# Self attention with one more score bank and shared transpose banks, and matrix products without use at pauses

## The reference, cut to what matters

```python
# x [1,512,512], ctx [1,8192,512]; 16 heads of 32, D = 512
x = x + xattn(layernorm(x), ctx)          # softmax(q k^T / sqrt(32)) v, 8192 keys, then Wo
x = x + attn(layernorm(x))                # below, 512 keys
x = x + ffn(layernorm(x))                 # 8 experts, 2 per token, 512 -> 1024 -> 512

def attn(x):
    Q, K, V = (split_heads(x @ W.T) for W in (W_Q, W_K, W_V))
    Q, K = layernorm(Q, q_ln_w, q_ln_b), layernorm(K, k_ln_w, k_ln_b)
    attn = softmax(Q @ K.T / sqrt(32)); context = attn @ V
    z = context_flat @ sparse_W_V.mean(axis=2)            # one number for each row and head
    y = top_k(z, 128)  outer  sparse_W_O.mean(axis=1)
    return y @ W_O.T
```

## Time and profile before

| | us |
|---|---|
| median of 3 runs | 1608.14 (1606.55 to 1609.6) |
| the profiled execution | 1605.24 |
| its span, first to last instruction | 1603.5 |
| mean granted clock of PE | 0.973 |
| PE busy | 1507.0 |
| DVE busy | 1252.5 |
| ACT busy | 1039.9 |
| POOL busy | 410.2 |

### The profile page before, as it was taken

One profiled execution on the slowest core, in us unless ns is written; L12 is line 12 of the kernel. 1 busy time (PEld: TensorE's weight loads), 2 busy tenths in 40 slices (PEclk: granted clock), 3 DMA queues, 4 the chain that ended last, 5 costly groups with the idle time before them and its releaser, 6 DMA issues. The chain is left out here.

```text
span 1603.5 us, 23326 instructions
## 1 busy us (share of the span) xinstructions
PE 1507.0 (94%) x8494; PEld 845.5 (53%) x8494; DVE 1252.5 (78%) x1884; ACT 1039.9 (65%) x1343; POOL 410.2 (26%) x225
## 2 busy tenths in 40 slices
PE   6799999999999989999999999999988864899998
PEld 4466666666666533333333333333345631699996
DVE  5677776776777879999999999999885668477664
ACT  3366666666666778888888888888547841244441
POOL 5455545636556011404000400100005320100002
PEclk9899999999999989999999999999999986799999
DMA  4454444444544455455545445444156036399994
GB/s 183 158 197 145 171 171 139 177 161 155 179 155 152 132 145 132 113 151 165 140 123 143 121 115 123 115 123 120 38 84 128 2 128 247 106 326 348 363 340 138
DMA packets 119776, 254.55 MB, mean 159 GB/s; under 512 B 10152, under 2 KB 26536, under 8 KB 115184
## 3 DMA queue, kind: packets, MB, share of 16 engines
q1 hardware_dynamic: 117632, 248.35, 49.7%
q0 software_dynamic: 1408, 4.46, 0.9%
q10 hardware_dynamic: 624, 0.27, 0.1%
HBM read 182.26 MB, written 61.34 MB: 152 GB/s over the span
## 5 line engine op out<-in xcount | busy, mean ns | idle before, releaser
L772 ACT ACTIVATE att_pr<-b_sc 128x1024 f32<-128x1024 f32 x512 | 496.2, 1022 | 77.1 <-PE b_sc L676 77.1
L822 DVE TENSOR_TENSOR att_tot<-att_tot,att_pr 128x2048 f32<-128x2048 f32 x200 | 466.9, 2335 | 23.1 <-ACT att_pr L772 2.3
L497 DVE CUSTOM_DVE_ANT_0 ctx_size<-ctx_tot,ctx_size 128x512 f32<-128x512 f32 x512 | 332.9, 688 | 133.4 <-PE ctx_tot L411 129.7
L462 ACT ACTIVATE ctx_size<-ctx_dif 128x1024 f32<-128x1024 f32 x256 | 262.2, 1024 | 121.6 <-PE ctx_dif L411 121.6
L676 PE MATMUL b_sc<-g_stacks,att_kst 98*128 98x512 f32 x1024 | 309.1, 424 | 2.0 <-DMA att_kst<-keys_scratch 2.0
L676 PEld LDWEIGHTS b_sc<-g_stacks,att_kst 98*128 98x128 f32 x1024 | 173.8, 189 | 237.3 <-ACT att_pr L772 211.5
L690 PE MATMUL b_o<-att_pr,att_val 128*32 128x512 f32 x2048 | 273.6, 606 | 2.0 <-issue 1.9
L411 PE MATMUL ctx_dif<-ctx_k_dif,f_q_hi 32*128 32x512 f32 x512 | 128.5, 499 | 6.6 <-DVE ctx_k_sum L481 2.8
L411 PE MATMUL ctx_tot<-ctx_k_sum,f_q_hi 32*128 32x512 f32 x512 | 128.0, 497 | 0.0
L86 PE MATMUL f_proj<-f_wv_hi,g_stacks 128*128 128x512 f32 x320 | 120.8, 420 | 0.0
L86 PE MATMUL f_proj<-g_stacks,f_wk_hi 128*128 128x512 f32 x352 | 119.5, 420 | 0.5 <-DVE f_k_lo L206 0.5
(11 more groups left out here) (302 smaller groups left out, 2106.4 us busy)
## 6 DMA issues: line engine op xcount, KB each, us to landing
m_w<-in_W SPq DMA_DIRECT2D x30, 2048.0 KB, 10.6
att_kst<-keys_scratch SPq DMA_DIRECT2D x192, 256.0 KB, 3.9
f_raw<-in_ctx SPq DMA_DIRECT2D x32, 1024.0 KB, 6.1
keys_scratch<-f_k_hi SPq DMA_DIRECT2D x32, 512.0 KB, 2.8
keys_scratch<-f_k_lo SPq DMA_DIRECT2D x32, 512.0 KB, 3.2
values_scratch<-ctx_v SPq DMA_DIRECT2D x32, 512.0 KB, 3.2
att_val<-values_scratch SPq DMA_DIRECT2D x64, 256.0 KB, 2.7
rows_scratch<-mix_blank SPq DMA_DIRECT2D x1, 3840.0 KB, 23.7
```

The source lines that it names most:

```text
L462: act.activation(size[:, i % ABS, :], dif[:, :], ACT.Abs).then_inc(s_size, 1)
L497: dve.tensor_tensor_reduce(out=size[:, i % ABS, r * CH:(r + 1) * CH], in0=tot[i % 2][:, r * CH:(r + 1) * CH], in1=size[:, i % ABS, r * CH: ...
L772: act.activation(pr[:, T % SLOTS, 2 * s:2 * s + 2, :], sc[(2 * T + s) % PAIRS][:, :].rearrange("p (j q) -> p j q", j=2), ACT.Exp, scale=SC ...
L822: dve.tensor_tensor(tot[b % 2][:, :, :], so_far, pr[:, T % SLOTS, :, :], ALU.add).then_inc(s_add, 1)
```

## The change

`keep_warm` issues matrix products whose results nobody reads. It is called at the end of `project_context` (8 products of 512 columns, single-pass type), at the start of `attend_context` (16, and 4 more after `turn`; fp32, 128 columns), before and between the first `turn_rows` there (7 and 5), at the end of `self_attend` (4, fp32, 512 columns), and twice in `mix_and_route`: before the rank products (3, fp32, 512 columns) and after the last transposes (2).

In `self_attend` there are four `full` banks instead of three, three `tp` banks which the transposes of the sums share in turn (`turned` lists who gets a bank in which order), one `o` bank, and no `rs`. ACT's list becomes exp(i), copy(i-2). The head that DVE copies is j = 1. `invert` and PE's `shares` come one step earlier in their lists, ACT's `shares` two and `take` five. The last `shares` runs before the last `weighted`.

```diff
+def keep_warm(pe, out, left, right, times):
+    for _ in range(times):
+        pe.matmul(out, left, right, start=True, stop=True)
...
+            pe.wait_ge(s_size, STEPS)
+            keep_warm(pe, dif[:, 0:CH], c.wv_hi[:, 0, 0:P], c.wv_hi[:, 0, :], 8)
...
+            keep_warm(pe, den[:, 0:P], c.ident[:, :], c.ident[:, :], 16)
             pe.wait_ge(s_shift, 4)
             turn(pe, sc[0])
+            keep_warm(pe, den[:, 0:P], c.ident[:, :], c.ident[:, :], 4)
...
+            keep_warm(pe, den[:, 0:P], c.ident[:, :], c.ident[:, :], 7)
             turn_rows(0)
+            keep_warm(pe, den[:, 0:P], c.ident[:, :], c.ident[:, :], 5)
             turn_rows(1)
...
-    FULL = 3
+    FULL = 4
     KEPT = 3
+    BANKS = 3
+    LAG = 2
+    LATE = HG + 1
...
-        tp = [pb(f"tp{n}", [P, N]) for n in range(2)]
-        o = [pb(f"o{n}", [P, N]) for n in range(2)]
-        rs = pb("rs", [P, N])
+        tp = [pb(f"tp{n}", [P, N]) for n in range(BANKS)]
+        o = pb("o", [P, N])
...
         def by_vector(i):
-            return i % HG == HG - 1
+            return i % HG == 1
...
+        turned = []
+        for i in range(ALL):
+            turned.append(("head", i))
+            if i % STEPS == 1 and i > STEPS:
+                turned.append(("share", i // STEPS - 1))
+        turned.append(("share", G - 1))
+        def bank(kind, n):
+            return tp[turned.index((kind, n)) % BANKS]
+        def bank_free(engine, kind, n):
+            at = turned.index((kind, n)) - BANKS
+            if at >= 0:
+                kind, n = turned[at]
+                if kind == "head":
+                    moved_out(engine, n)
+                else:
+                    engine.wait_ge(s_share, n + 1)
...
             def turn(i):
                 pe.wait_ge(s_exp, i + 1)
-                if i >= 2:
-                    moved_out(pe, i - 2)
+                bank_free(pe, "head", i)
...
             def weighted(unit):
-                if t == 0 and g >= 2:
-                    pe.wait_ge(s_take, g - 1)
+                if t == 0 and g >= 1:
+                    pe.wait_ge(s_take, g)
...
                 turn(i)
-                if i % HG == 1 and i > HG:
-                    weighted(i // HG - 1)
-                if i % STEPS == 2 and i > STEPS:
+                if i % STEPS == 1 and i > STEPS:
                     shares(i // STEPS - 1)
+                if i >= LATE and (i - LATE) % HG == 0:
+                    weighted((i - LATE) // HG)
+            shares(G - 1)
             weighted(G * NT - 1)
-            shares(G - 1)
+            keep_warm(pe, full[0][:, :], c.swvT[:, 0, 0:P], c.swvT[:, 0, :], 4)
...
-                if i and not by_vector(i - 1):
-                    move(i - 1)
-                if i % STEPS == 4 and i > STEPS:
+                if i >= LAG and not by_vector(i - LAG):
+                    move(i - LAG)
+                if i % STEPS == 2 and i > STEPS:
                     shares(i // STEPS - 1)
+            for i in range(ALL - LAG, ALL):
+                move(i)
...
-                if n % STEPS == 2 and n > STEPS:
+                if n % STEPS == 1 and n > STEPS:
                     invert(n // STEPS - 1)
-                if n % STEPS == 9 and n > STEPS:
+                if n % STEPS == 4 and n > STEPS:
                     take(n // STEPS - 1)
-            move(ALL - 1)
+            move(ALL - HG + 1)
...
+            keep_warm(pe, yp[1][:, :], c.swoT[:, 0, 0:P], c.swoT[:, 0, :], 3)
             pe.wait_ge(s_set, 8)
...
             mm.then_inc(s_turned, 1)
+            keep_warm(pe, yp[1][:, :], c.swoT[:, 0, 0:P], c.swoT[:, 0, :], 2)
```

More of the change, by code:

```diff
@@ L1168, in moved_out @@
             else:
[L1169 removed]
+                engine.wait_ge(s_even, (HG - 1) * (i // HG) + (1, 1, 2, 3)[i % HG])
+        turned = []
[14 more added lines that the diff above has]
+                    engine.wait_ge(s_share, n + 1)
         @block.sync
@@ L1190, in turn @@
                 pe.wait_ge(s_exp, i + 1)
-                if i >= 2:
-                    moved_out(pe, i - 2)
+                bank_free(pe, "head", i)
                 for u in range(NT):
-                    mm = pe.transpose(tp[i % 2][:, u * P:(u + 1) * P], prob[:, i % KEPT, u * P:(u + 1) * P], c.ident[:, :])
+                    mm = pe.transpose(bank("head", i)[:, u * P:(u + 1) * P], prob[:, i % KEPT, u * P:(u + 1) * P], c.ident[:, :])
                 mm.then_inc(s_tp, 1)
@@ L1213, in shares @@
                 pe.wait_ge(s_wide, g + 1)
-                if g:
-                    pe.wait_ge(s_share, g)
+                bank_free(pe, "share", g)
                 for t in range(NT):
-                    mm = pe.transpose(rs[:, t * P:(t + 1) * P], wide[:, g % 2, t * P:(t + 1) * P], c.ident[:, :])
+                    mm = pe.transpose(bank("share", g)[:, t * P:(t + 1) * P], wide[:, g % 2, t * P:(t + 1) * P], c.ident[:, :])
                 mm.then_inc(s_rs, 1)
@@ L1242, in move @@
                     act.wait_ge(s_pv, unit - 1)
-                act.activation(pr[unit % 2][:, i % HG, :], tp[i % 2][:, :], ACT.Copy).then_inc(s_even, 1)
+                act.activation(pr[unit % 2][:, i % HG, :], bank("head", i)[:, :], ACT.Copy).then_inc(s_even, 1)
             def shares(g):
@@ L1249, in shares @@
                     act.wait_ge(s_take, g)
-                act.activation(share[:, :], rs[:, :], ACT.Copy).then_inc(s_share, 1)
+                act.activation(share[:, :], bank("share", g)[:, :], ACT.Copy).then_inc(s_share, 1)
             for i in range(ALL):
@@ L1324, in move @@
                     dve.wait_ge(s_pv, unit - 1)
-                dve.tensor_copy(pr[unit % 2][:, i % HG, :], tp[i % 2][:, :]).then_inc(s_odd, 1)
+                dve.tensor_copy(pr[unit % 2][:, i % HG, :], bank("head", i)[:, :]).then_inc(s_odd, 1)
             def invert(g):
@@ L1342, in take @@
                     dve.wait_ge(s_place, SPOTS * (g - 1))
-                dve.tensor_tensor(held[:, g % 2, :], o[g % 2][:, :], share[:, :], ALU.mult).then_inc(s_take, 1)
+                dve.tensor_tensor(held[:, g % 2, :], o[:, :], share[:, :], ALU.mult).then_inc(s_take, 1)
             for n in range(ALL):
```

4 lines of the change are left out of this document (2 added, 2 removed).

## The result

The changed kernel takes 1594.41 us, the median of 4 runs (1590.27 to 1597.44), against 1608.12 us before (4 runs, 1606.55 to 1609.6): 0.9903 of the time, 95% interval 0.9881 to 0.9924. Its profiled execution took 1590.27 us, with a span of 1588.6 us. The forecast was 1589.5 us, range 1583 to 1600. The measured median lies inside this range, 4.9 us above the forecast.

The account below looks back on a forecast made before the run. DVE bounds the context attention; self attention is held by late score products, other stages by PE's low clock. 11.3 + 1.4 - 0.2 + 0.9 + 0 + 3.2 + 1.0 = 17.6 us off 1605.24 gives 1587.6, median 1589.5, range 1583 to 1600.

Parts of the forecast that it names:

- the first two rivals: Clock products give nothing, only self attention gains (0.17, about 1594.5); another chain takes over in self attention (0.12, about 1595).
- Self attention: Fourth score bank lets units run at ACT's pace, 4.11 instead of 4.89 us; 63 steps take 68.2, gain 11.3.
- The bound of 12.9: Upper bound of self attention's gain, without stalls and cold steps: 12.9 us.
- the 6 for units of 4.4: Lower bound of self attention's gain: 6 us if units only come to 4.4.
- Moving DVE's copy costs nothing: Self attention: DVE's copy moves from head 3 to head 1, the same copy in a list with 0.7 us spare.
- The tail: End of self attention: inverse sums go ahead of the weighted product, `take` at 3.3 instead of 4.76 us; gain 1.4.
- Start of mixing: First half of eight instructions ahead of DVE's maxima runs at the high clock: gain 0.9, between 0 and 1.1.
- Route products: Three products before the rank end 1.0 late, rank instructions give 1.1 back: zero, between -2.4 and +1.1; last two nothing.
- Experts: Start of the experts at the high clock, first hidden product 4.1 earlier, then rows' DMA: gain 3.2, between 0 and 4.1.
- Context attention: Its start: 16 products delay transposes 1.4, but DVE's 1.01 us stall and slow weighted product go: +1.0, between -5 and +2.
- The median: New median put 1.9 us above the forecast execution of 1587.6, instead of 2.9, as products should reduce differences between runs.
- the rival that I built on the rule: Cycling through more banks makes the clock swing in self attention, low for half the units: 1618 us; chance 0.03.

Follow-up runs that it names:

- the kernel with the early products: Changed kernel plus 26 more products without use between 43 and 54 us, ahead of the context attention's block: 1592.68 us, 0.9887 of before.
- the bank part: Changed kernel without any of the products without use, self attention as changed: 1596.84 us, 0.9928 of the time before.
- the last round: Changed kernel once more, nothing altered, beside a kernel with further products and a second copy on DVE: 1593.94 us, ratio 0.9888.

## Why the prediction was right, point by point

The number alone proves little: the median of 1594.4 lies outside my forecast's own range of 1585 to 1593, and right at the values of the first two rivals (1594.5 and 1595). It is the blocks that tell them apart. The mechanism came as forecast in self attention, and the products did give something at the experts. That the sum of the blocks is near, 18.9 us for 17.6, is in part luck: self attention gave 1.7 more than forecast and the experts 0.8 less.

**Self attention** was to give 11.3 and gave 13.2 (63 steps in 66.28 us, 79.47 before): right mechanism, with the extras set too high. The unit was forecast at 4.11 from ACT's pitches and came at 4.08. What was mis-sized are the extras: I charged 1.5 for the share copies, 1.2 for the group ends and 0.8 for the slow start, 3.5 together, on top of 64.7 for the units. Measured, 15.75 units of 4.08 are 64.3, so the extras come to 2.0. A group end, with its share copy, costs 4.68 + 4.17 - 2 x 4.08 = 0.69 (the first of the three 0.55), and the first four units take 15.92 instead of 16.32, because the first copies come two steps late; that pays for the slow start (the clock was at 0.50 from 1222 to 1224 us). The bound of 12.9 that I gave as without stalls and cold steps does not follow from my own terms: 11.3 + 1.2 + 0.8 is 13.3, and the gain stays just under it. Nor does the 6 for units of 4.4, which by the same terms is 6.7. PE's 3.80 us a unit was wrong too, with no effect on the time: it is 4.0. The steps of the earlier trace rows were right, but from the last transposes' start to the weighted product it takes 0.6 us, not half a step.

**"Moving DVE's copy costs nothing"** is true beside the lag and false alone. As an argument it was too short: I counted DVE's list and not what the free place does to ACT's.

**The tail** was to give 1.4 and gave 1.1 (3.68 us from the last exponential to `take`, 3.3 forecast). The last weighted product starts 2.54 us after the last exponential, where I had 2.1. The four products behind it run to 1294.87, ACT's last copy to 1294.63; from the last exponential to the next block it is 7.51 us, 7.43 without products. So they cost 0.1, forecast 0.2.

**Start of mixing**: 0.9 forecast, 0.9 measured: DVE's first MAX8 starts 1.79 us after the block's start, 2.69 before.

**Route products**: forecast at zero, done at 1374.6 on the old scale, 1.0 late. They took 4.52 us, with the clock at 0.59 in the stretch from 1358 to 1360 us. The rank started 67.0 us after the block's start, against 66.0 in the kernel without them, and its first eight instructions ran in 0.95 us instead of 1.84. The times came as written. My reason for the clock being down, that the small products ahead leave PE little to do, does not fit the trace of the kernel before: PE was busy for 1.76, 1.70 and 2.00 us of the three stretches of 2 us from 1364 to 1370, with the clock at 1.00, and it was down right behind. What I had not seen is that these products carry the experts' gain, nor that the last two, which I had at nothing, cost 1.9 us if they run at the low clock.

**Experts** was the step that failed in size: 3.2 forecast, 2.4 measured. The first hidden product was to come 7.5 us after the first bias product and came 9.2 after (11.6 before): the own rows took 5.46 and not 3.6, as the clock fell again under them. So the wait for the rows' DMA behind it did not appear in the changed kernel; in the kernel with the early products it did, with 0.90 us. My landing time was 0.2 early by my own rows (1391.27 + 3.3 is 1394.6).

**Context attention**: +1.0 forecast, 1.2 measured. Of the parts, the first scores come 6.4 us after the block's start, 5.3 before, waiting for their DMA, and the first exponential 0.6 later than before, where I had no change; DVE's stall of 1.01 us ahead of its second sum is gone, and 1.8 us are gained behind the first exponential. Beside the bank part (606.6) it is 3.3, of which 1.7 are the fall of the clock near that block's end. The 7 and 5 products before `turn_rows`, which I had at zero, stand in just these pauses; the kernel before has none and its clock held there, so what they give is not shown. In two of 11 profiles with the 16 products the clock fell all the same and the block took 0.7 and 1.6 longer than before: inside my range of -5 to +2, but the +1.0 holds for the other nine alone.

**The median.** I put it 1.9 above the sum and it is 6.8 above. This is the term that was most off, and it rested on a guess: that the products take away part of the difference between runs. That is not seen: the six runs of the changed kernel in the last round spread over 13.1 us, the eleven of the kernel before over 6.2. The profiles show three chances of this size: the first block (569 to 574 us over the 14 profiles); the mixing block, 71.1 and 72.6 us in the two profiles of the changed kernel, where the clock fell behind the last logits or ahead of them, and up to 74.3 in the other kernels; and the context attention, 602.7 to 606.0 with the same 16 products. The 8 products at the first block's end neither cause nor mend this. Runs of 1597 to 1599 are longer than any profiled execution of this kernel, and what they consist of stays open.

The Trainium skill's "TensorE: Matmul & The Clock Gate", section "A second HAM failure mode: psum-queue depth-cycling", spoke for a clock that swings in a stage that cycles through its banks. The changed kernel's self attention cycles through four score and three transpose banks, and the row of 1222 to 1288 us above has 0.98, with the low clock only in its first four microseconds (0.50, then 0.69). The trace does not agree, and the rival that I built on the rule did not come.

## What to carry to other kernels

Before a bank is added, write down each engine's list around the product that is late, and move the copies as well: here the new bank layout alone was worth 0.32 us a unit, with the copies one step later 0.81, and the same copies with three score banks nothing. Products that only keep the clock up belong where a chain that sets the end follows a pause, and each place has to be measured in several profiles: all of them together gave 1 to 5 us, at the context attention the clock fell all the same in two profiles of 11, and at the route two of them cost 1.9 us when they ran at the low clock. When a run of the changed kernel gives less than its stages, compare blocks that were not changed before looking for a cause in those that were.

## What the runs showed of the hardware that was not expected

The clock can fall while PE is busy without a break. In the changed kernel's second profile it was 0.88 and then 0.50 under the logits' products of 8 columns (here the timeline, and below it the stretches of that kernel), and 16 of them took 3.42 us. In the first profile the clock held under the same instructions, and they took 1.91:

```profile
1352.67 3.42 PE L1515 MATMUL mix_acc<-m_wg,g_hT 128*128 128x8 f32 x16
```

```profile
1351.00:1353.00 2.00, 2.00 (x19) 2.00 (x18) 0.71 (x2) 0.75 (x3) 0.00 (x0) 0.88 0.00 0
1353.00:1355.00 2.00, 2.00 (x11) 2.00 (x10) 0.00 (x0) 1.79 (x2) 0.00 (x0) 0.50 0.00 0
```

The same is seen from 1368 us on in the first profile (0.65, then 0.50, PE busy throughout), behind products that use 8 of the 128 rows. What decides it is not shown by these runs.

And the keys' first DMA at the context attention, which the first scores wait for, varies from profile to profile: they start 5.3, 5.8 and 7.4 us after the block's start in the three profiles in which the transposes start at 2.2, and 5.8 to 7.0 in the 11 in which they start at 3.7.
